# A delta attention in chunks of 32 tokens, and eight experts written out as one sequence

## The chip, the cores and the metric

One core of one Trainium2 chip runs the whole program. The metric is the time on the device in microseconds (us), the median of several executions. Everything is four-byte floating point. A core has five engines, each with an instruction stream of its own: TensorE (PE) multiplies matrices, VectorE (DVE) and ScalarE (ACT) work on elements, GpSimd (POOL) does elementwise work too, and SyncE (SP) starts transfers. They wait for each other by semaphores. On PE each product of four-byte numbers stands in the trace as two matmul records and two weight-load records (PEld); the count of products in the program order is therefore half of the records. A transpose on PE leaves one record of each kind.

## The reference

Four layers, each an attention and a feed-forward part with layernorms and residuals, run over 4 sequences of 1024 tokens and 128 channels (32 tiles of 128 tokens). Two parts matter here. The feed-forward part of layer 2:

```
logits = x @ gate_w.T                  # 8 experts
mult, sel = _sparse_mixer_top2(logits) # two experts per token and their weights
h1, h3 = x @ w1[e].T, x @ w3[e].T      # 256 wide, every expert for every token
out = sum_e weight[t, e] * ((silu(h1) * h3) @ w2[e].T)
```

The attention of layer 3 (4 heads of 32 channels): q, k and v are projections with a convolution of 4 taps and silu; v also goes through convolutions of 7 and of 25 taps; a delta rule runs in chunks of 32 tokens:

```
T = I + strictly lower part, so that T = inverse(I + tril(beta k k^T, -1))
u_i = T v_i - T k_i S                  # per chunk of 32 tokens
o_i = q_i S + tril(q_i k_i^T) u_i
S   = S + k_i^T u_i
```

The four paths (two convolutions, the delta rule's output, v itself) are then mixed by a small router network.

## The kernel before, in words

The program is a row of stages. A stage (`Stage`) allocates buffers and semaphores, has one block with a function for each engine, and ends in a barrier of all engines (`end_step`). Inside a block each engine runs its instructions in the order in which they are written; there is no scheduler. So the order of the code is the order on each engine.

**The experts, `l2_ffn_stage` (L2267 on).** After the weights are loaded and turned, a hardware loop (`nc.Fori`) makes 8 passes, each over 512 tokens. A pass copies its columns of `XNT` to `xs` (ACT), multiplies them with the gate (PE, `logits`), and on VectorE finds the two best experts and their weights in some thirty small operations on 32 columns. Then come 8 experts: for each half k of the hidden width PE makes `h1` and `h3` (128x512), ACT the tanh `th`, VectorE `gated` and `act`; `second_product` makes `y` in 8 products of 128x128; `gather` adds it with its weight to `acc` on VectorE. `h1`, `h3` and `y` have two buffers each. The last operation adds `acc` to `X`. Every pass begins when the pass before it is over on all engines.

**The preparation, `l3_paths_steps` (L2498 on).** It runs once for each of the four sequences: projections (PE), copies (ACT), convolutions of 4 taps (VectorE, one operation of 128x1024 for each tap), silu, then on VectorE the convolution of 7 taps into `lm[:, 0]`, the sums of squares for the norms (`sums`, from small products on PE), reciprocal, the scaled keys `kn_tok`, and the convolution of 25 taps into `lm[:, 1]`. PE turns these to token rows, ACT copies them to `outs`.

**The chunk stage, `l3_chunk_steps` (L2627 on).** It runs once for each pair of sequences (`a3d0`, `a3d1`), after the preparation of the two. A step takes the next 128 tokens of both. Phase q of a step builds a 128x128 gram per head and sequence (`big`), masks it to `N`, cuts out its 32x32 diagonal blocks `Nc`, makes five masked levels `lev` (POOL), and grows the inverse: `SMALL`-1 = 4 rounds on 32x32 blocks in which PE makes `zt`, ACT copies it to `Zt`, PE makes both the new `T` (`tps`) and its transpose (`xps`), VectorE adds them; then two rounds join the blocks to 64 and to 128 (`T64`, `Zt6`, `x5`, `x6`). Phase r takes the previous 128 tokens: `kS`, `R`, `u` (with 128x128 stationary `XT`), the output, and the state `S`, a 128x128 matrix of which only the heads' blocks are kept (`dS`). There are 8 blocks of 128 tokens, so 9 steps.

Of the kernel before, what the change touches and what calls it, by code (L numbers as in the profile page):

```python
# [2266 lines left out]
def l2_ffn_stage(nc, X, XNT, c, gate_w, w1, w2, w3):  # L2267


    with Stage(nc, "f2") as outer:  # L2270
# [11 lines left out]
        with Stage(nc, "f2s") as st:  # L2282
            xs = st.sb("xs", [P, G * P])
            lg, size, gap, first, second, rest = (st.sb(n, [P, G, EXPERTS]) for n in
                                                  ("lg", "size", "gap", "first", "second", "rest"))
# [4 lines left out]
            atf = st.sb("atf", [P, G, 8])  # L2290
            total, mult = (st.sb(n, [P, 2, G]) for n in ("total", "mult"))
# [3 lines left out]
            acc = st.sb("acc", [P, G, P])  # L2295
            logits = st.ps("logits", (P, G, EXPERTS))
            h1 = st.ps("h1", (P, 2, 512))
            h3 = st.ps("h3", (P, 2, 512))
            y = st.ps("y", (P, 2, G, P))
            s = st.sems("xs_ready logits_ready shifted1 exps h1_ready h3_ready th_ready act_ready y_ready y_used "  # L2300
                        "added chain")
            with nc.Fori(0, TILES // G) as i:
                with nc.Block(no_gpsimd_drain=True) as block:
                    @block.scalar
                    def _(a):
                        a.activation(xs[:], XNT[:, ds(i * G * P, G * P)], ACT.Copy).then_inc(s["xs_ready"], 1)
                        a.wait_ge(s["shifted1"], 1)
                        a.activation(ex1[:], ex1[:], ACT.Exp)
                        a.activation(ex2[:], ex2[:], ACT.Exp).then_inc(s["exps"], 1)
                        for n in range(2 * EXPERTS):  # L2310
                            a.wait_ge(s["h1_ready"], n + 1)
                            if n >= 2:
                                a.wait_ge(s["act_ready"], n - 1)
                            a.activation(th[:, n % 2, :], h1[:, n % 2, :], ACT.Tanh, scale=0.5).then_inc(s["th_ready"], 1)
# [1169 lines left out]
```

## Time and profile before

| | |
|---|---|
| median of 3 executions | 8866.54 us (8864.33 to 8873.16) |
| the profiled execution: time / its span | 8869.6 us / 8867.9 us |
| VectorE busy in the experts' stretch 6901 to 7337 | 300 of 436 us |
| 25-tap and 7-tap operations on VectorE (128x1024) | 120 of 1285 ns |
| preparation 7366 to 7442: VectorE / PE busy | 59.6 / 26.8 of 76 us |
| PE waits put to "issue" in 7517 to 7875 | 48.7 us in 40 waits, longest 2.1 us |

Times in the trace count from the span's start. "[1.46 <-issue]" behind an instruction says that its engine had been idle for 1.46 us before it, and what ended the idle time; "issue" means that nothing recorded was waited for. PEclk is the granted clock of PE as a share of 2.4 GHz: 0.5 is its lower level of 1.2 GHz. The experts, the four preparations and the two chunk stages together lie between 6899 us and 8385 us of the span; nothing of another stage runs beside them.

### The profile page before, as it was taken

The page shows a single profiled execution, that of the slowest core. Times are in us where ns is not written, and L with a number is a line of the kernel's source. Part 1 is how long each engine was busy: PE and PEld are TensorE (multiplying, and loading weights), DVE is VectorE, ACT ScalarE, POOL GpSimd, SP SyncE. Part 2 cuts the span into 40 slices and gives each one's busy share as a digit, 9 for nine tenths or more (in the row PEclk, how much of TensorE's full clock was granted, in tenths as well). Part 3 has the DMA queues.
Part 4 walks back from the last instruction along what each step waited for, and adds up shares of the span by engine and source line. Part 5 has one row for each costly group of instructions (what it writes and reads, how often), then busy time and mean ns, then how long its engine had stood idle before and what let it go on. Part 6 is the DMA issues. An engine that isn't in the chain of part 4 may idle for free. (4 is left out here: it accounts for less than half of the span.)

```text
span 8867.9 us, 296237 instructions
## 1 busy us (share of the span) xinstructions
PE 7434.6 (84%) x129602; PEld 5365.8 (61%) x129602; DVE 5896.1 (66%) x11053; ACT 4141.6 (47%) x6986; POOL 2935.6 (33%) x2152
## 2 busy tenths in 40 slices
PE   7999699999996998988988998998986784756666
PEld 3443588888885665665665665666654453645534
DVE  6664477777776885876876866867865667253266
ACT  3554244444444775765765766756752121111121
POOL 0111022222223773764754755746730000101000
PEclk8998699999998998999999999999998895555556
DMA  0000000000001221221221222212210000000000
GB/s 14 1 1 1 5 5 5 5 5 5 5 3 40 70 73 43 69 72 40 73 65 47 70 59 56 71 50 63 72 30 5 9 0 2 3 2 2 4 0 12
DMA packets 192069, 256.75 MB, mean 29 GB/s; under 512 B 59957, under 2 KB 86452, under 8 KB 189876
## 3 DMA queue, kind: packets, MB, share of 16 engines
q1 hardware_dynamic: 190772, 237.70, 10.1%
q8 instruction: 1029, 16.86, 0.8%
q14 instruction: 268, 2.20, 0.1%
HBM read 27.84 MB, written 2.10 MB: 3 GB/s over the span
## 5 line engine op out<-in xcount | busy, mean ns | idle before, releaser
L1764 PE MATMUL wa_front<-w_wqkv,wa_xsT 128*128 128x512 f32 x2000 | 994.8, 621 | 40.1 <-PEq L66 20.3
L1686 POOL TENSOR_TENSOR XNT<-XNT 128x1024 f32<-128x1024 f32 x396 | 937.8, 2368 | 251.2 <-DVE XNT L1870 251.2
L1689 POOL TENSOR_TENSOR XNT<-XNT,wa_rnorm 128x1024 f32<-128x1024 f32 x330 | 627.9, 1903 | 361.9 <-DVE wa_rnorm L1878 361.9
L1867 DVE TENSOR_TENSOR XNT<-wa_front,w_scaled 128x1024 f32<-128x1024 f32 x330 | 393.5, 1192 | 311.1 <-ACT wa_sq L1705 228.8
L1764 PEld LDWEIGHTS wa_front<-w_wqkv,wa_xsT 128*128 128x128 f32 x2000 | 346.3, 193 | 316.9 <-issue 297.4
L446 PE MATMUL a0h_ring<-a0h_QT,a0h_KT 32*128 32x512 f32 (+3 forms) x1536 | 457.5, 567 | 14.2 <-ACT a0h_E L564 10.4
L564 ACT ACTIVATE a0h_E<-a0h_ring 128x512 f32<-128x512 f32 (+1 forms) x640 | 320.6, 555 | 296.7 <-PE a0h_ring L446 295.1
L1705 ACT ACTIVATE wa_sq<-wa_front 128x1024 f32<-128x1024 f32 x335 | 340.1, 1015 | 182.5 <-PE wa_front L1764 182.5
L1870 DVE TENSOR_TENSOR XNT<-wa_front,w_scaled 128x512 f32<-128x512 f32 x660 | 421.0, 679 | 0.0
L1883 DVE TENSOR_REDUCE wa_norm<-wa_sq 128x16 f32<-128x1024 f32 x330 | 398.5, 1207 | 0.0
L1770 PEld LDWEIGHTS wa_front<-consts,XNT 128*128 128x128 f32 x2640 | 299.0, 142 | 124.7 <-issue 62.3
L1770 PE MATMUL wa_front<-consts,XNT 128*128 128x128 f32 x2640 | 357.1, 278 | 14.7 <-POOL XNT L1689 6.9
L1348 POOL TENSOR_TENSOR a1s_Estrict<-a1s_E,a1s_sb 128x512 f32<-128x512 f32 x64 | 81.2, 1269 | 861.3 <-ACT a1s_E L1286 861.3
L437 PE MATMUL a0h_slots<-a0h_KT,a0h_QT 32*128 32x512 f32 (+3 forms) x1536 | 349.1, 559 | 8.6 <-DVE a0h_part L643 3.4
L1908 DVE TENSOR_TENSOR wa_o<-wa_back,wa_rtotal 128x1024 f32<-128x1024 f32 x165 | 202.0, 1224 | 210.9 <-PE wa_back L1826 210.9
L2817 POOL TENSOR_TENSOR a3d_sb<-consts,a3x_nbeta 128x1024 f32<-128x1024 f32 x16 | 31.0, 1937 | 926.9 <-POOLq L66 926.9
L1852 PE MATMUL wa_back<-w_wo,wa_oT 128*128 128x128 f32 x2640 | 330.5, 280 | 5.6 <-ACT wa_oT L1750 5.6
L606 POOL TENSOR_SCALAR_AFFINE_SELECT a0h_E<-a0h_E 128x512 f32<-128x512 f32 x128 | 79.7, 635 | 755.3 <-ACT a0h_E L564 755.3
L1692 POOL TENSOR_TENSOR wa_sc<-wa_sc,wa_smax 128x1024 f32<-128x1024 f32 x160 | 304.3, 1902 | 70.5 <-DVE wa_smax L1921 70.5
L1852 PEld LDWEIGHTS wa_back<-w_wo,wa_oT 128*128 128x128 f32 x2640 | 315.6, 196 | 7.6 <-ACT wa_oT L1750 7.6
L1826 PEld LDWEIGHTS wa_back<-wa_v_look,wa_pT 64*32 64x32 f32 x21120 | 223.0, 106 | 154.3 <-issue 146.9
L1379 DVE SCALAR_TENSOR_TENSOR a1s_conv<-a_hist,a_taps,a1s_conv 128x512 f32<-128x512 f32 x384 | 303.9, 791 | 11.2
(659 smaller groups left out, 19547.7 us busy)
## 6 DMA issues: line engine op xcount, KB each, us to landing
wa_v_look<-wa_v_all SPq DMA_DIRECT2D x990, 128.0 KB, 2.4
wa_v_look<-wa_v_all SPq DMA_DIRECT2D x660, 64.0 KB, 2.0
wal_v_look<-wal_v_all SPq DMA_DIRECT2D x198, 128.0 KB, 2.4
wal_v_look<-wal_v_all SPq DMA_DIRECT2D x132, 64.0 KB, 2.0
w_wqkv<-in_L_ffn_Wqkv_dram SPq DMA_DIRECT2D x6, 1024.0 KB, 6.4
w_wo<-in_L_ffn_Wo_dram SPq DMA_DIRECT2D x6, 512.0 KB, 6.9
w_wqkv<-in_L_ffn_Wqkv_dram SPq DMA_DIRECT2D x12, 256.0 KB, 7.9
f2w_raw<-in_L_ffn_w_dram SPq DMA_DIRECT2D x48, 64.0 KB, 1.9
```

The costliest lines, as they stand in the source:

```text
L437: last = pe.matmul(o[:, i, at:at + w], QT[rows, n % 2, t * P:(t + 1) * P], KT[rows, n % 3, k * 512:k * 512 + w], start=True, stop=True)
L446: last = pe.matmul(o[:, at:at + w], KT[rows, n % 3, kb * P:(kb + 1) * P], QT2[rows, k, 512 - w:512], start=True, stop=True)
L564: a.activation(E[:, m % 3, j, 0:w], ring_of(key)[:, 0:w], ACT.Exp).then_inc(s["ring_a"], 1)
L1686: g.tensor_tensor(rot[:, at], rot[:, at], part[:, at], ALU.add).then_inc(s[summed], 1)
L1689: g.tensor_tensor(rot[:, at], rot[:, at], spread(rnorm[:, at, :], HDW), ALU.mult).then_inc(s[done], 1)
L1705: a.activation(sq[:, n].rearrange("p h d -> p (h d)"), two_banks(front, bank[n]), ACT.Square).then_inc(s[done], 1)
L1764: last = pe.matmul(front[:, first + i, :], xsT[:, slot, :], wqkv[:, (2 * n + i) * 512:(2 * n + i + 1) * 512], start=True, stop=True)
L1770: last = pe.transpose(front[:, first + i // 4, (i % 4) * P:(i % 4 + 1) * P], rot[:, n, 2 * i:2 * i + 2, :].rearrange("p h d -> p (h d)"), ...
L1852: last = pe.matmul(back[:, 0, 0:P], oT[:, i, :], wo[:, i, :], start=(i == 0), stop=(i == INNER // P - 1))
L1867: v.tensor_tensor(rot[:, n], src, cos, ALU.mult)
L1870: last = v.tensor_tensor(part[:, n, :, p0:p0 + 32], src[:, :, p1:p1 + 32], sin[:, :, p0:p0 + 32].broadcast_to([P, H, 32]), ALU.mult)
L1883: v.tensor_reduce(norm[:, n, :], sq[:, n], AX.X, ALU.add).then_inc(s[norm_in], 1)
```

## The change

Three things change.

1. **Experts.** No loop over passes: one block holds 64 units of work (8 groups of 512 tokens by 8 experts) in a row, all reading `XNT` itself. The gate products of all 32 tiles come first, then one routing on 256 columns for all tokens. `y` has three buffers, `gather` adds straight into `X` and stands between the two halves of a later unit.
2. **Preparation.** Keys and values are turned by head (`turn_heads`: 128 products of 32x32 each), the sums of squares come as 8 + 128 + 128 products, the norms' operations stand inside the 25-tap convolution (behind its taps 14 and 18), and the keys stay unscaled: `bp` = beta/|k|^2 takes the norm in.
3. **Chunk stage.** One stage for all four sequences, with chunks of 32 tokens. Partition quarters are heads; a step has M = 16 matrices per quarter (4 chunks by 4 sequences). Gram and scores are one set of 64 products of 32x64 (`gq`). The inverse is `XT` alone, grown 4 times by one set (`xps`); VectorE's 32x32 transpose gives `T` from `XT` (`turn`), so that `tps` and the rounds to 64 and 128 go. The state is 32x32 per head and sequence, carried chunk by chunk (`look`, `solve`, `learn`, 4 times in a step); the output is turned at the step's end (`oT`).

The core of the diff:

```
-            with nc.Fori(0, TILES // G) as i:
+            work = [(g, e) for g in range(NG) for e in range(EXPERTS)]
...
+                    for i in range(len(work)):
+                        hidden(2 * i)
+                        if i >= 2:
+                            gather(i - 2)
+                        hidden(2 * i + 1)
...
-            turn(rawp[:, 0], qk[:, 1, k], s["tok_ps"])
+            turn_heads(rawp[:, 0], qk[:, 1, b], s["ktok_ps"])
...
+            convolve(act[:, 2, :], vh[:], wide_taps[:, LOCAL:], MID, {14: sums, 18: scales}).then_inc(s["path_ready"], 1)
...
-                        blocks_of(tps, XTc, lambda p, m: Zt[p, m, :], s["t_ps"])
-                        blocks_of(xps, Zt, lambda p, m: XTc[p, m, :], s["x_ps"])
+                    each(every, whole(xps), whole(Zt), whole(XT[:, q % 2])).then_inc(s["x_ps"], 1)
...
+                    each(every, lambda p, m: gq[p, m, :, :], chan(1, q),
+                         lambda p, m: qk[p, :, m % BATCH, tokens(q, m)]).then_inc(s["gq_ps"], 1)
+                for n in range(PER):
+                    look(n)
+                    zt(n + 1)
+                    solve(n)
+                    grow(n + 1)
+                    learn(n)
...
+                def turn():
+                    v.wait_ge(s["X_ready"], LX * q + turns + 1)
+                    if LV * q + turns >= 1:
+                        v.wait_ge(s["zt_ps"], LV * q + turns)
+                    v.transpose(columns(T[:]), columns(XT[:, q % 2])).then_inc(s["T_ready"], 1)
...
+                g.wait_ge(s["N_ready"], q + 1)
...
+                for n in range(SMALL):
+                    g.tensor_tensor(lev[:, n], N[:], small[:, n:n + 1, :].broadcast_to(tiny), ALU.mult).then_inc(s["lev_ready"], 1)
```

How it stands on the engines, at three places. First PE in the chunk stage; before, from the last round on 32x32 blocks (`ztp`, `tps`, `xps`) over the joining rounds to the next step's gram and state products (`big`, `rec`):

```order
L2666 MATMUL a3d_ztp<-a3d_T,a3d_lev 32x32 x32
L2666 MATMUL a3d_tps<-a3d_Zt,a3d_XTc 32x32 x32
L2666 MATMUL a3d_xps<-a3d_XTc,a3d_Zt 32x32 x32
L2691 MATMUL a3d_ztp<-a3d_T,a3d_N 32x32 x16
L2718 MATMUL a3d_tps<-a3d_Zt,a3x_XT 32x32 x8
L2722 MATMUL a3d_xps<-a3x_XT,a3d_Zt 32x32 x16
L2699 MATMUL a3d_ztp<-a3x_T,a3d_N 64x64 x8
L2728 MATMUL a3d_xps<-a3x_XT,a3d_Zt 64x64 x8
L2739 MATMUL a3d_big<-a3x_qk 128x128 x8
L2746 MATMUL a3d_rec<-a3x_S,a3x_qk 128x128 x2
L2753 MATMUL a3d_rec<-a3d_R,a3x_XT 128x32 x8
```

and now, in the middle of a run of steps, from the output's transposes over the gram-and-score set to the first state update (`kps` and the first `ops` are `look`, `ups` is `solve`, `sps` and the second `ops` are `learn`):

```order
L2755 MATMUL a3d_ztp<-consts,a3d_oT 128x128 x4
L2673 MATMUL a3d_gq<-a3x_qk 32x64 x64
L2673 MATMUL a3d_kps<-a3d_S,a3x_qk 32x32 x16
L2673 MATMUL a3d_ops<-a3x_qk,a3d_S 32x32 x16
L2673 MATMUL a3d_ztp<-a3d_T,a3d_lev 32x32 x64
L2673 MATMUL a3d_ups<-a3d_R,a3d_XT 32x32 x16
L2673 MATMUL a3d_xps<-a3d_XT,a3d_Zt 32x32 x64
L2673 MATMUL a3d_sps<-a3d_u,XN 32x32 x16
L2673 MATMUL a3d_ops<-a3d_AT,a3d_u 32x32 x16
```

The joining rounds are gone, and the state's products stand between the inverse's in each of the four rounds. A full step of before has 510 products, in 14 such steps and two half ones; now one has 896 and 4 transposes (64, and 4 times the 208 from `kps` to the second `ops`), in 7 such steps; the first step has 576 (no state), the last 320 and 4 transposes (no inverse). Second, VectorE in the preparation, before from the 7-tap convolution on:

```order
L2592 SCALAR_TENSOR_TENSOR a3p_lm<-a3p_vh,a3x_wide_taps,a3p_lm 128x1024 x6
L2610 TENSOR_SCALAR a3p_sums<-a3p_rawp 128x8x2x4
L2612 TENSOR_SCALAR a3x_beta<-a3p_tb 128x32
L2613 TENSOR_SCALAR a3x_nbeta<-a3p_tb 128x32
L2615 RECIPROCAL a3x_rnorms<-a3p_sums 128x64
L2617 TENSOR_TENSOR XN<-a3p_rawp,a3x_rnorms 128x1024
L2590 TENSOR_SCALAR a3p_lm<-a3p_vh,a3x_wide_taps 128x1024
L2592 SCALAR_TENSOR_TENSOR a3p_lm<-a3p_vh,a3x_wide_taps,a3p_lm 128x1024 x24
```

and now:

```order
L2604 SCALAR_TENSOR_TENSOR a3p_act<-a3p_vh,a3x_wide_taps,a3p_act 128x1024 x14
L2623 TENSOR_SCALAR a3x_rnq<-a3p_rawp 128x32
L2624 TENSOR_SCALAR a3p_ss<-a3p_rawp 128x32
L2625 TENSOR_SCALAR a3p_tb<-a3p_tb 128x32
L2604 SCALAR_TENSOR_TENSOR a3p_act<-a3p_vh,a3x_wide_taps,a3p_act 128x1024 x4
L2629 RECIPROCAL a3p_ss<-a3p_ss 128x32
L2630 TENSOR_TENSOR a3x_bp<-a3p_tb,a3p_ss 128x32
L2631 TENSOR_SCALAR a3x_nbp<-a3x_bp 128x32
L2632 RECIPROCAL a3x_rnq<-a3x_rnq 128x32
L2634 TENSOR_TENSOR a_outs<-a3p_rawp,a3p_root 128x8x128
L2604 SCALAR_TENSOR_TENSOR a3p_act<-a3p_vh,a3x_wide_taps,a3p_act 128x1024 x6
```

The small operations that wait for PE's sums stood ahead of the 25-tap convolution and stand inside it now. Third, VectorE at the experts' beginning, where the two experts of each token are found, before, in each of 8 passes:

```order
L2350 COPY f2s_lg<-f2s_logits 128x32
L2352 MAX f2s_top<-f2s_lg 128x8 x4
L2355 MAX_INDEX f2s_at<-f2s_top,f2s_lg 128x8 x4
L2357 TENSOR_SCALAR f2s_size<-f2s_lg 128x32
L2358 CAST f2s_atf<-f2s_at 128x32
L2359 TENSOR_TENSOR f2s_size<-f2s_size,f2s_lg 128x32
```

and now, once:

```order
L2348 COPY f2s_lg<-f2s_logits 128x256
L2350 MAX f2s_top<-f2s_lg 128x8 x32
L2353 MAX_INDEX f2s_at<-f2s_top,f2s_lg 128x8 x32
L2355 TENSOR_SCALAR f2s_size<-f2s_lg 128x256
L2356 CAST f2s_atf<-f2s_at 128x256
L2357 TENSOR_TENSOR f2s_size<-f2s_size,f2s_lg 128x256
```

Eight small routings have become one wide one ahead of all 64 units. Behind it, a unit's instructions on PE and VectorE are those of an expert before, except that the weighted sum stands between the two halves of a unit.

## Rows read from the trace of the kernel before

**Rows 1.** Busy time by stretch; columns: us, each engine's busy time, PEclk, DMA share, GB/s.
```profile
6901.00:7337.00 436.00, 374.94 (x1600) 233.69 (x1600) 300.30 (x856) 91.05 (x159) 0.00 (x0) 0.92 0.00 0
...
6970.00:6985.00 15.00, 15.00 (x72) 9.70 (x71) 10.64 (x23) 2.98 (x5) 0.00 (x0) 0.99 0.00 0
...
8025.00:8384.00 359.00, 259.61 (x8156) 236.55 (x8156) 91.36 (x198) 42.96 (x104) 39.41 (x24) 0.51 0.01 3
```

**Rows 2.** Timeline, experts, even running: start us, us, engine, line, operation, count [idle<-releaser].
```profile
6921.27 1.95 PE L2329 MATMUL f2s_y<-f_w2T,f2s_act 128*128 128x128 f32 x16
...
6926.49 1.95 PE L2329 MATMUL f2s_y<-f_w2T,f2s_act 128*128 128x128 f32 x16
```

**Rows 3.** Timeline of the experts: second pass up to its first activation; stage behind them.
```profile
6956.44 1.88 PE L2320 MATMUL f2s_logits<-f_gT,f2s_xs 128*128 128x8 f32 x8 [5.33 <-ACT f2s_xs L2306]
...
6958.58 0.37 DVE L2352 MAX8 f2s_top<-f2s_lg 128x8 f32<-128x8 f32 x4
...
6959.66 0.18 DVE L2357 TENSOR_SCALAR f2s_size<-f2s_lg 128x32 f32<-128x32 f32 x1
...
6965.06 0.69 DVE L2392 SCALAR_TENSOR_TENSOR f2s_gated<-f2s_th,f2s_h 128x512 f32<-128x512 f32 x1
...
7337.28 1.28 ACT L167 ACT_TABLE_LOAD   x1 [6.92 <-PEq L66]
```

**Rows 4.** The gate products of all eight passes, by tile: ns, first and last start.
```profile
L2320 PE MATMUL f2s_logits<-f_gT,f2s_xs x64: 256/361/382, 6901.3 to 7287.0; 128*128 128x8 f32 x64
```

**Rows 5.** Timeline, preparation of the first sequence.
```profile
7388.66 1.94 PE L2518 MATMUL a3p_rawp<-consts,a3x_qk 128*128 128x128 f32 x8 [15.32 <-DVE a3x_qk L2603]
...
7402.36 0.23 DVE L2610 TENSOR_SCALAR a3p_sums<-a3p_rawp 128x64 f32<-128x64 f32 x1 [2.73 <-ACT a3p_tb L2568]
...
7403.85 0.55 DVE L2615 RECIPROCAL a3x_rnorms<-a3p_sums 128x64 f32<-128x64 f32 x1 [1.09 <-ACT a3p_sums L2570]
...
7438.07 1.97 PE L2518 MATMUL a3p_mid<-consts,a3p_lm 128*128 128x128 f32 x8 [28.68 <-DVE a3p_lm L2592]
```

**Rows 6.** Timeline, where chunk stages begin and the stages behind them begin.
```profile
7517.98 1.24 PE L2739 MATMUL a3d_big<-a3x_qk 32*128 32x128 f32 x16 [2.02 <-PEq L66]
...
7873.81 4.55 PE L2523 MATMUL a3p_rawp<-XNT,a3x_proj 128*128 128x512 f32 x5 [1.64 <-PEq L66]
...
8025.55 1.24 PE L2739 MATMUL a3d_big<-a3x_qk 32*128 32x128 f32 x16 [1.97 <-PEq L66]
...
8384.94 0.33 SPq L2932 DMA_DIRECT2D a3y_rw1a<-in_L_attn_r_w_dram  x1
```

**Rows 7.** Timeline of TensorE in the second chunk stage, dense 32x32 products.
```profile
8306.57 0.26 PE L2666 MATMUL a3d_ztp<-a3d_T,a3d_lev 32*32 32x32 f32 x8 [1.46 <-issue]
...
8310.14 0.34 PE L2666 MATMUL a3d_xps<-a3d_XTc,a3d_Zt 32*32 32x32 f32 x9 [1.45 <-issue]
8310.27 1.06 PE L2666 MATMUL a3d_ztp<-a3d_T,a3d_lev 32*32 32x32 f32 x64
8311.83 0.96 PE L2666 MATMUL a3d_tps<-a3d_Zt,a3d_XTc 32*32 32x32 f32 x55 [0.50 <-ACT a3d_Zt L2805]
8313.63 0.37 PE L2666 MATMUL a3d_tps<-a3d_Zt,a3d_XTc 32*32 32x32 f32 x9 [0.83 <-issue]
...
8321.21 0.27 PE L2666 MATMUL a3d_xps<-a3d_XTc,a3d_Zt 32*32 32x32 f32 x5 [1.46 <-issue]
```

**Rows 8.** The page, busy time and instructions of each engine, then its queues.
```profile
PE 7434.6 (84%) x129602; PEld 5365.8 (61%) x129602; DVE 5896.1 (66%) x11053; ACT 4141.6 (47%) x6986; POOL 2935.6 (33%) x2152
...
q8 instruction: 1029, 16.86, 0.8%
```

**Rows 9.** Timeline, GpSimd's masks in a chunk step.
```profile
7604.36 0.72 POOL L2824 TENSOR_TENSOR a3d_lev<-a3d_Nc,a3x_small 128x256 f32<-128x256 f32 x1 [38.97 <-ACT a3d_Nc L2792]
7605.04 2.35 POOL L2825 TENSOR_TENSOR a3d_lev<-a3d_Nc,a3x_small 128x1024 f32<-128x1024 f32 x1
```

**Rows 10.** Groups by line in the experts: xcount, busy us, mean ns, idle us, releaser.
```profile
L2314 ACT ACTIVATE f2s_th<-f2s_h 128x512 f32<-128x512 f32 x128 | 75.4, 595 | 234.5 <-PE f2s_h L2338 234.5
```

More of the change, by code:

```diff
@@ L2425 @@
+            st.end_step()
 HEADS3 = 4
@@ L2474, in _ @@
             def _(v):
-                v.memset(XT[:], 0.0)
-                v.memset(T64[:], 0.0)
+                for i, mask in enumerate((c.strict, c.upto)):
+                    for h in range(HEADS3):
+                        v.tensor_copy(within[quarter(h), i, 0, :], mask[quarter(h), quarter(h)])
                 v.wait_ge(s["loaded"], 160)
@@ L2508, in l3_paths_steps @@
     mine = slice(b * BLOCKS, (b + 1) * BLOCKS)
+    QS, KS, BS = (slice(n * CHUNKS3, (n + 1) * CHUNKS3) for n in range(3))
     def by_tile(ap):
@@ L2519, in turn, with turn_heads @@
                 last.then_inc(sem, 1)
+            def turn_heads(out, src, sem):
+                for n in range(CHUNKS3):
+                    at = slice(n * CHUNK3, (n + 1) * CHUNK3)
+                    for h in range(HEADS3):
+                        last = pe.matmul(out[quarter(h), at], src[quarter(h), at], c.ident[quarter(h), quarter(h)], start=True,
+                                         stop=True)
+                last.then_inc(sem, 1)
             for n in range(3):
@@ new lines, in grow, with look @@
+                    pe.wait_ge(s["zt_ready"], LV * q + n)
+                    pe.wait_ge(s["X_ready"], LX * q + n)
+                    each(every, whole(xps), whole(Zt), whole(XT[:, q % 2])).then_inc(s["x_ps"], 1)
+                def look(n):
+                    if r is None:
+                        return
+                    k = PER * r + n
+                    ms = range(n * BATCH, (n + 1) * BATCH)
+                    pe.wait_ge(s["S_ready"], k + 1)
+                    each(ms, per_batch(kps), chan(1, r), per_batch(S)).then_inc(s["k_ps"], 1)
+                    if n == 0 and r >= 1:
+                        pe.wait_ge(s["o_kept"], r)
+                    each(ms, whole(ops), per_batch(S), chan(0, r), first=ms[0], end=M)
@@ L2781, in _ @@
+                if r is not None:
+                    pe.wait_ge(s["o_kept"], r + 1)
+                    if q is not None:
+                        pe.wait_ge(s["zt_ready"], LV * (q + 1))
+                    for b in range(BATCH):
+                        last = pe.transpose(ztp[:, b * BATCH:(b + 1) * BATCH, :].rearrange("p a e -> p (a e)"), oT[:, b, :], c.ident)
+                    last.then_inc(s["turned"], 1)
         @block.scalar
```

714 lines of the change are left out of this document (312 added, 402 removed).

## The prediction

> **What bounds the kernel now.** I read the busy times by stretch first. Three stretches matter, one after the other with barriers between: the experts (6899 to 7337 us), four preparations of a sequence (about 76 us each) and two chunk stages. Among the experts PE is at 15.00 of 15 us once it runs evenly, at the upper clock level (granted 0.99), but over all passes at 375 of 436 us and 0.92 [rows 1]. In the chunk stage PE is at 260 of 359 us at the lower level (0.51), VectorE at 91, so no engine is full there: the reader has to ask what each round waits for. The timelines give that.
>
> Experts: one expert costs 5.22 us, from one `y` to the next [rows 2]. A pass takes (7287.0 - 6901.3)/7 = 55.1 us [rows 4], 8 x 5.22 = 41.8 of it work; the other 13.3 are the copy to `xs`, the gate products, VectorE's routing (6958.35 to 6965.06) and the restart of PE at the lower clock level [rows 3].
>
> Preparation: VectorE is the chain. It waits twice for PE's and ACT's small sums, 2.73 and 1.09 us [rows 5].
>
> Chunk stage: between its 32x32 sets PE is idle for "issue", 0.8 to 1.5 us each time [rows 7]. Between two such gaps stand 9 + 64 + 55 = 128 matmul records, that is 64 products, each time the same. The page has 129602 matmul and as many load records and 1029 packets of instructions of 16.4 KB each [rows 8]: 252 records to a packet, so a packet is about 64 products. PE has used up its instructions and waits for the next packet. From gap end to gap end it takes 3.57 us, and over four such intervals 8306.57 to 8321.21, 3.66 each [rows 7], the last two of them 3.79. The 64 products themselves take no more than 1.7 us (64 records in 1.06 us, their tail of 0.2 included), and ACT waits of 0.5 us that fall inside an interval do not lengthen it. So dense small products come at one packet per 3.66 us, whatever PE could do. Before, only five of the eight packets of a step (510 products) are that dense; the rest of its 45 us (359.4/8, [rows 6]) is a chain of waits.
>
> At this place a rule speaks against me. The Trainium skill, page "Runtime: NRT & Kernel Launch", section "Instruction fetch mechanics", says that the sequencer fetches the next 16 KiB block of 256 instructions while it runs the present one, that crossing a block is "mostly hidden", and that kernels prefer full unrolling. Size and count of a block agree with the trace; hidden it is not, by gaps of 0.8 to 1.5 us. By the rule the chunk stage would end earlier; that is the first rival below.
>
> **Chunk stage, worked out.** Removed: both stages, 7517.98 to 7873.81 and 8025.55 to 8384.94 [rows 6], 355.8 + 359.4 = 715.2 us. Added, in packets of 64 products: the first step 576 products, seven steps of 896 and 4 transposes, the last 320 and 4.
> - A full step is 14.03 packets, at 3.66 that is 51.4 us. Does the chain fit below? A set of 64 products takes 1.75 us plus 0.2 tail (twice the 64 records above). ACT's 512-wide copy costs 0.60 [rows 10], a 512-wide VectorE operation 0.69 [rows 3]. A round: `look` 0.9, `zt` 1.75, tail, copy and handovers 0.95, `grow` 1.75 + 0.25, VectorE's add 0.7, transpose 0.7, state 0.3 + 0.1: 7.4 us for 208 products, whose 3.25 packets take 11.9. So it fits and the fetch sets the pace; `solve` and `learn` lie beside the copies.
> - VectorE's 32x32 transpose has no row. Below it can't be free, since it reads and writes 512 columns; I take 0.7, as the 512-wide operations. From above, the slowest VectorE row by element is the reciprocal, 0.55 us for 64 columns [rows 5], which would be 4.4 us for 512: the round becomes 11.1 and still fits, the first step (128 products to a round, 7.3 us by packets, then 9.9 by chain) does not: + 10 there and + 4 at each full step's start, + 38 in all. The Trainium skill, "VectorE: DVE Perf Modes", section "The three transpose paths", has 311 ns for 128x128 of two bytes; four times that is an estimate of 1.2 us, and no term would change by it.
> - A step's start does not fit wholly: `gq`, then mask `N` 0.7, POOL's first level (256 columns take 0.72, 1024 take 2.35 [rows 9], so about 1.3 for 512), identity 0.7, transpose 0.7, handovers 0.4: 4 us in which PE has only `look` (0.9) to do. With the packet of `gq` itself, that is 1 us over the packets' time, and the wait for the copy before the output's transposes adds 1. I take 53.5 for a full step; bounds 51.4 (all hidden) and 60 (below). The added waits are `zt`'s for the levels and the transposes' for `o_kept`; behind both stands the whole next set of PE.
> - Sum: first step 9 packets + 1.5 = 34.5; 7 x 53.5 = 374.5; last step 5.03 packets = 18.4, then copy 0.8, transposes 0.9, scaling 0.8, barrier 1.3: 22.3. Together 431.3. Gain 715.2 - 431.3 = 283.9 us. POOL has 7.5 us of work in a step, and VectorE about 12: neither bounds.
>
> **Experts, worked out.** Gone: seven starts. New: gate products of 32 tiles, 64 records; at the lower level 8 take about 1.7 us [rows 3], all 14.2; at the upper, by `y`'s 16 in 1.95 [rows 2], 7.2. The clock rises on the way, I take 10. Then routing: maximum and index of 4 tiles take 6958.58 to 6959.66, 1.08 us [rows 3], 8 times that is 8.6; 21 further operations of 256 columns, between 0.22 each (like the 32-wide) and 0.69 (512-wide), midway 0.45: 9.5; copy 0.3. Together 18.4 (13.5 to 23.4). Then 64 units: first activation to first `y` 6.7, 62 x 5.22 = 323.6, the last two `y` 3.6, the last sum 1.3: 335.3. Barrier 1.2. From 6899.4 on: 10.2 + 18.4 + 335.3 + 1.2 = 365.1, end at 7264.5 where it was 7337.28 [rows 3]: gain 72.8, bounds 63 to 81. Nothing new binds in a unit: the second half's activation ends about 5.7 us after PE has begun the unit, PE asks for it at 6.9. The `xs` copy, its table load and the add into `X` go with the passes.
>
> **Preparation, worked out.** VectorE loses the waits of 2.73 and 1.09 us and starts its 25 taps at 7399.6; `sums` comes behind 0.75 + 14 x 1.285, at 7418.4. PE needs to have: 128 products by head from 7388.66 [rows 5] (two packets, 5.5 to 7.3 us), 8 wide ones 3.4, 256 small ones (four packets 14.6, up to 20.7): 7412 to 7420. Then 8 transposes 2, 128 products 5.5 to 7.3: 7420 to 7429, where `scales` asks at 7424.9. So 25 taps end 4.2 us earlier or up to 4 later than that; I take 3.5 us gained for each of four, 14 us, bounds 0 to 17. The cover is the 25 taps: without them the 14.6 us of packets would be on the path.
>
> **Sum.** Against the profiled execution's own 8869.6 us: 8869.6 - 283.9 - 72.8 - 14 = 8498.9. The median of the runs is 3.1 us lower: 8496 us.
>
> **The rivals.**
> 1. *The fetch is hidden, the chain bounds* (the page's rule). For: nothing but the "issue" gaps shows the fetch, and PE did run 215 records without one behind a slow stretch. Against: every dense stretch of every step has the gaps. Then a full step is 36.5 us (7.4 to the first `zt`, three rounds of 7.3, a last of 5.3, 1.9 for the output), the first 30, the last 17: 302 in place of 431. Time 8367 us. 12%.
> 2. *Waits and fetch add up.* If packets are asked for only as PE gets on, each round's own waits (0.5 for the copy, 1.1 for state and transpose) come on top: + 6.5 in a full step, 60 us, + 10 in the others. For: a packet is fetched only after the packet before is begun. Against: the 0.5 us waits inside the intervals of rows 7. About + 57: 8553 us. 14%.
> 3. *The transpose costs by element like the reciprocal:* + 38, 8534 us. 3%.
> 4. *Slower than before.* The place is the packet fetch: 112.2 packets in the chunk stage. If a fetch took twice as long, because PE's stream in one long stage runs ahead of nothing, 112.2 x 3.66 = 411 us more come on top, and the preparations' small products (384 more in each, 6 packets) outlast the 25 taps: about 8930 us. It decides from 3.66 + 371/112.2 = 7.0 us a packet on. Against: the longest pair of intervals in rows 7 is 3.79 each. 2%.
>
> **How the numbers follow.** My forecast has 69%: 8496, with its own range 8465 to 8530. Range: rival 2 and 3 fall within 8555; below, rival 1 is mostly left out, with the experts' and transposes' bounds I go to 8440. Faster by over 0.2% (18 us, about what a measurement can tell from no change) are all cases but the last: 0.97; no change 0.01; slower 0.02.
>
> **What would show it.** In the new profile: "issue" gaps on PE throughout the chunk stage, 128 matmul records apart, 3.6 to 3.7 us from end to end; full steps of 53 to 54 us; one stage of about 431. Among the experts, `y` every 5.22 us for 335 us at a clock of 0.99, ahead of it 28 to 29 us of gate products and routing. In the preparation, the last turn 3 to 4 us earlier. Wrong would be: no gaps and steps below 45 us (rival 1), steps near 60 with waits for VectorE between gaps (rival 2), `y` further apart than 5.3 us, or `scales` waiting for over 4 us.

## The result and the profile after

| | before | after |
|---|---|---|
| median | 8869.85 us (4 runs) | 8508.15 us (8501.87 to 8527.02, 4 runs) |
| after / before | | 0.9595, 95% interval 0.9578 to 0.9612 |
| predicted | | 8496, range 8440 to 8555 |
| profiled execution | 8869.6 us | 8527.0 us, span 8525.3 |

The change takes 362 us away; the prediction said 374. The profiled execution lies 19 us above the median: its expert stage begins 15.9 us later than in the profile of before (6915.2 against 6899.3), although the code ahead of it is the same. In the fourteen profiles of this case that point lies anywhere from 6880 to 6915 us. So a stage is compared by its own length, and stage lengths tell more than times of whole executions.

The page answers to [rows 8]: PE has 1960 matmul records more in all (fewer for the joining rounds, more for small products), and 26 instruction packets more.

```profile
PE 7158.4 (84%) x131562; PEld 5126.3 (60%) x131562; DVE 5768.2 (68%) x10639; ACT 4064.7 (48%) x6793; POOL 2917.3 (34%) x2152
...
q8 instruction: 1055, 17.29, 0.9%
```

Busy time by stretch, columns as in [rows 1]: the experts, and the seven full steps of the chunk stage. PE is now busy 350 of 366 us among the experts (375 of 436 before), and in the chunk stage still only 216 of 388, still near the lower clock level.

```profile
6914.00:7280.00 366.00, 350.31 (x1600) 224.76 (x1600) 253.09 (x634) 78.20 (x131) 0.00 (x0) 0.96 0.00 1
7633.00:8021.00 388.00, 215.84 (x12561) 195.64 (x12552) 86.66 (x168) 20.56 (x35) 52.39 (x41) 0.53 0.02 4
```

Timeline of the experts: gate products, their copy, VectorE's first activation behind the routing, two `y` in a row, and the first instruction of the stage behind. They answer to [rows 2, 3].

```profile
6915.23 11.54 PE L2316 MATMUL f2s_logits<-f_gT,XNT 128*128 128x8 f32 x64 [1.27 <-PEq L66]
...
6926.81 0.42 DVE L2348 COPY f2s_lg<-f2s_logits 128x256 f32<-128x256 f32 x1 [12.52 <-PE f2s_logits L2316]
...
6943.49 0.69 DVE L2389 SCALAR_TENSOR_TENSOR f2s_gated<-f2s_th,f2s_h 128x512 f32<-128x512 f32 x1
...
6950.21 1.95 PE L2326 MATMUL f2s_y<-f_w2T,f2s_act 128*128 128x128 f32 x16
...
6955.43 1.95 PE L2326 MATMUL f2s_y<-f_w2T,f2s_act 128*128 128x128 f32 x16
...
7280.10 1.28 ACT L167 ACT_TABLE_LOAD   x1 [6.32 <-PEq L66]
```

Gate products 11.5 us (10 predicted), routing 16.7 from the copy to the first activation (18.4), units and last sum 335.7 (335.3), `y` every 5.22. From its first instruction, a table load of ScalarE at 6915.19, to the first of the next stage it takes 7280.10 - 6915.19 = 364.9 us (365.1), against 437.9 before: 73.1 us gained (72.8).

VectorE in the preparation, in answer to [rows 5]: the first tap, `sums`, `scales`, and the first tap of the next sequence. Neither `sums` nor `scales` has idle time ahead of it.

```profile
7313.74 0.75 DVE L2600 TENSOR_SCALAR a3p_act<-a3p_raw,a3x_taps 128x1024 f32<-128x1024 f32 x1 [4.70 <-ACT a3p_raw L2565]
...
7361.56 0.19 DVE L2623 TENSOR_SCALAR a3x_rnq<-a3p_rawp 128x32 f32<-128x32 f32 x1
...
7367.13 0.35 DVE L2629 RECIPROCAL a3p_ss<-a3p_ss 128x32 f32<-128x32 f32 x1
...
7385.95 0.76 DVE L2600 TENSOR_SCALAR a3p_act<-a3p_raw,a3x_taps 128x1024 f32<-128x1024 f32 x1 [4.70 <-ACT a3p_raw L2565]
```

One sequence to the next: 72.2 us, before 75.9. The gain of 3.7 us each was predicted as 3.5. PE's last gates and last turned values, on which the two depend:

```profile
7354.18 0.70 PE L2548 MATMUL a3p_rawp<-a3x_wb,XNT 128*32 128x1 f32 x37 [1.86 <-issue]
...
7361.12 0.68 PE L2523 MATMUL a3p_rawp<-consts,a3p_vh 32*32 32x32 f32 x45 [1.95 <-issue]
```

The small products are done at 7354.9, 6.7 us before `sums` asks, and the values by head at 7361.8, 5.3 us before `scales`.

TensorE in the first step of the chunk stage, up to the second step's first product. It answers to the starts in [rows 6]:

```profile
7597.45 3.36 PE L2673 MATMUL a3d_gq<-a3x_qk 32*32 32x64 f32 x128 [1.97 <-PEq L66]
7605.57 1.93 PE L2673 MATMUL a3d_ztp<-a3d_T,a3d_lev 32*32 32x32 f32 x128 [4.76 <-DVE a3d_T L2806]
...
7612.47 1.93 PE L2673 MATMUL a3d_ztp<-a3d_T,a3d_lev 32*32 32x32 f32 x128 [1.72 <-DVE a3d_T L2806]
...
7632.53 0.30 PE L2673 MATMUL a3d_gq<-a3x_qk 32*32 32x64 f32 x3
```

No state is looked at here, so each round has 128 products; from one `ztp` to the next it takes 6.9 to 7.4 us, and the waits for `T` show between them: this step is in the main a chain of waits. A full step has both, a wait at its start and packets behind it. The rows are: the last packet of the step before, this step's `gq`, VectorE's addition of the identity and its transpose, the first `ztp`, then four gaps (three that follow each other, and the ninth behind them):

```profile
7797.33 0.32 PE L2673 MATMUL a3d_ops<-a3d_AT,a3d_u 32*32 32x32 f32 x5 [1.54 <-issue]
...
7799.39 3.10 PE L2673 MATMUL a3d_gq<-a3x_qk 32*32 32x64 f32 x128
...
7804.64 1.74 DVE L2850 TENSOR_TENSOR a3d_XT<-a3d_lev,a3x_small 128x512 f32<-128x512 f32 x1 [0.58 <-POOL a3d_lev L2789]
...
7806.40 0.71 DVE L2806 STREAM_TRANSPOSE a3d_T<-a3d_XT 128x512 f32<-128x512 f32 x1
...
7807.22 1.93 PE L2673 MATMUL a3d_ztp<-a3d_T,a3d_lev 32*32 32x32 f32 x128 [4.14 <-issue]
...
7811.44 1.65 PE L2673 MATMUL a3d_xps<-a3d_XT,a3d_Zt 32*32 32x32 f32 x106 [1.06 <-issue]
...
7815.19 0.37 PE L2673 MATMUL a3d_sps<-a3d_u,XN 32*32 32x32 f32 x10 [1.82 <-issue]
...
7818.53 1.65 PE L2673 MATMUL a3d_ztp<-a3d_T,a3d_lev 32*32 32x32 f32 x107 [1.16 <-issue]
...
7853.46 0.44 PE L2673 MATMUL a3d_ops<-a3d_AT,a3d_u 32*32 32x32 f32 x16 [1.81 <-issue]
```

The gap of 4.14 us ahead of 7807.22 carries the word "issue" too, but it is a wait for `T`: the transpose ends at 7807.11, and the first `ztp`, which reads `T`, begins 0.1 us later. It does so in each of the seven full steps, and 180 records, not 128, lie between this row and the next gap. The other gaps are those of packets. From 7811.44 to 7853.46 there are 11 intervals of 128 records (127 in some), 42.0 us, 3.82 each. Over all intervals of 128 records in the seven full steps the mean is 3.74, and 3.63 to 3.67 in four other profiles of the same stage; in [rows 7] it was 3.66. The three packets from 7797.33 to 7811.44, over the step's start, take 14.1 us. Last, where the step without an inverse begins, and the next stage:

```profile
8022.44 0.65 PE L2673 MATMUL a3d_kps<-a3d_S,a3x_qk 32*32 32x32 f32 x32
...
8042.24 0.33 SPq L2903 DMA_DIRECT2D a3y_rw1a<-in_L_attn_r_w_dram  x1
```

The chunk stage takes 8042.24 - 7597.45 = 444.8 us, where the two of before took 715.2; predicted were 431.3. PE's waits in the seven full steps (us in total, times, longest):

```profile
PE a3d_ztp L2673 <- issue: 63.0, 29, 4.1
PE a3d_xps L2673 <- issue: 39.3, 28, 2.2
...
PE a3d_kps L2673 <- DVE a3d_S L2832: 10.2, 11, 0.9
PE a3d_xps L2673 <- ACT a3d_Zt L2767: 5.4, 20, 0.3
PE a3d_ztp L2755 <- ACT a3d_oT L2772: 4.2, 6, 0.7
PE a3d_ztp L2673 <- DVE a3d_T L2806: 3.9, 1, 3.9
```

With the groups left out, 148 of 172 us of idle time are put to "issue". But 24 of these are six of the waits for `T` at a step's start, 3.6 to 4.1 us each; for the seventh the profile names `T` (3.9). So 124 us are left for the packets, and handovers come to 47 us, 6.8 a step, four of them at the start. VectorE's and GpSimd's operations on 512 columns, by tile, with the shortest, median and longest in ns:

```profile
L2806 DVE STREAM_TRANSPOSE a3d_T<-a3d_XT x32: 711/711/712, 7604.7 to 8007.6; 128x512 f32<-128x512 f32 x32
...
L2850 DVE TENSOR_TENSOR a3d_XT<-a3d_lev,a3x_small x8: 1731/1734/1735, 7602.9 to 7971.7; 128x512 f32<-128x512 f32 x8
...
L2789 POOL TENSOR_TENSOR a3d_lev<-a3d_N,a3x_small x40: 1256/1263/1718, 7601.6 to 7975.7; 128x512 f32<-128x512 f32 x40
```

The transpose, for which no row of before stood, takes 0.711 us (0.7 was taken). The addition of the identity (L2850) takes 1.73 us where 0.7 was taken. GpSimd's level takes 1.26 (1.3 was taken).

### The profile page after: what moved, and what is told of

The parts are those of the page before. It is cut to its first block and busy times, and to the rows that moved or that the text cites. A ratio compares the mean times of both kernels' runs of the same rounds, so it can differ in the third digit from the quotient of the medians.

```text
span 8525.3 us, 299038 instructions
## 1 busy us (share of the span) xinstructions
PE 7158.4 (84%) x131562; PEld 5126.3 (60%) x131562; DVE 5768.2 (68%) x10639; ACT 4064.7 (48%) x6793; POOL 2917.3 (34%) x2152
## 5 line engine op out<-in xcount | busy, mean ns | idle before, releaser
L446 PE MATMUL a0h_ring<-a0h_QT,a0h_KT 32*128 32x512 f32 (+3 forms) x1536 | 457.3, 567 | 14.2 <-ACT a0h_E L564 10.4
L1379 DVE SCALAR_TENSOR_TENSOR a1s_conv<-a_hist,a_taps,a1s_conv 128x512 f32<-128x512 f32 x384 | 304.3, 792 | 11.2
L643 DVE TENSOR_REDUCE a0h_part<-a0h_slots 128x2 f32<-128x1024 f32 (+3 forms) x256 | 257.3, 1021 | 78.5 <-PE a0h_slots L437 76.3
```

The costliest lines, as they stand in the source:

```text
L446: last = pe.matmul(o[:, at:at + w], KT[rows, n % 3, kb * P:(kb + 1) * P], QT2[rows, k, 512 - w:512], start=True, stop=True)
```

## Experiments

My theory: PE's instruction packets (16 KB, 256 instructions, that is 64 products of four-byte numbers) set the pace of the chunk stage, at a rate that neither the products' own time nor short waits change. Rival: its chain of waits does, with or without the packets' time on top. All names and shapes below are those of the changed kernel; "step" is a full step, a mean over the seven.

### Each part alone

The new `l2_ffn_stage` in the kernel before (`experts_alone`), and the old one in the changed kernel (`layer3_alone`); whole functions are exchanged.

> The kernel before with the new expert stage alone. My theory: the three parts add up, and this one is worth the 73.1 us that lie between the stage's start and its end in the two profiles (437.9 before, 364.9 after): 8870 - 73 = 8797 us. Rival: part of it belongs to what stands behind (code laid out elsewhere, a layernorm that begins at another clock level), then 8810 or more. In its profile the stage should again take 364 to 366 us, with a second product every 5.22 us.

Measured: ratio 0.9925 (0.9907 to 0.9942), 8791.7 us against 8854.0 on the same chip. The stage takes 7271.0 - 6903.1 = 367.9 us, 2 to 4 more than expected. Twelve profiles have this stage: in six it takes 364.9 us and the gate products 11.2 to 11.5, in the other six 367.9 to 368.0 and the gate products 13.8. So most of the 3 us lies in the gate products. Over them the granted clock is 0.50 in `experts_alone` and 0.61 in the changed kernel's profile; the prediction had 14.2 us for the lower clock level.

> The changed kernel with the old expert stage. My theory: 8870 - 270 (chunk stages 715.2 to 444.8) - 15 (preparations) = 8585 us. Rival: the parts depend on each other, for instance because the clock level carries over from the experts into the preparation; then the two savings measured alone differ from the whole, 362, by more than 8 us.

Measured: ratio 0.9689 (0.9666 to 0.9712), 8572.8 us. Chunk stage 435.5 us, preparations 288.3 from the first to the chunk stage (288.6 in the changed kernel, 303.4 before).

By the ratios the parts are worth 67 and 276 us, together 343, the whole 359. The difference of 16 us is more than the 8 that were set as the sign of a dependence; but each figure has an uncertainty of 15 to 20 us, so the totals neither show nor exclude one. The stages' own lengths are sharper: 70 to 73, 15, and 270 to 280 us.

### Fewer products, the same chain

```diff
-                    if n == 0 and r >= 1:
-                        pe.wait_ge(s["o_kept"], r)
-                    each(ms, whole(ops), per_batch(S), chan(0, r), first=ms[0], end=M)
```

> The changed kernel without the 16 products of q S in each round, 64 in each step with a state: this part of the output is left out; the chain of waits for the inverse and the state is the same. Fetch sets the pace: one packet of 64 products less in seven full steps and in the last, 8 x 3.66 to 8 x 3.85, 29 to 31 us less than the changed kernel (8508), 8477 to 8479, and full steps of 52.3 us where they take 56.3 now. Rival, the chain of waits sets it: these products stand beside VectorE's R, at most 0.43 us each round is PE's own time, 32 x 0.43 = 14 us at most and more likely none: 8494 to 8508.

The wait for `o_kept` that goes with them costs nothing: the transposes of the step before have waited for the same copy.

Measured: 8490.3 us (ratio 0.9580, 0.9561 to 0.9599, the changed kernel 0.9595); the stage 417.4 us, a step 52.0. Against three profiles of the unchanged stage (444.8, 435.5, and 436.3 in `after_again`; mean 438.9, step 54.8) that is 21.5 us less, 27.4 against the first alone. The same stage also stands in two runs below, `fetch_micro` (438.2) and `loop_sizes` (443.7); the mean of all five is 439.7, the step again 54.8. The gaps of TensorE stand as before:

```profile
7805.03 1.22 PE L2673 MATMUL a3d_xps<-a3d_XT,a3d_Zt 32*32 32x32 f32 x74 [0.70 <-issue]
...
7809.05 0.36 PE L2673 MATMUL a3d_ops<-a3d_AT,a3d_u 32*32 32x32 f32 x10 [2.10 <-issue]
```

8 packets of 3.7 would be 29 us, the rival's most is 14. Neither fits well: removed packets bring 2.7 us each. An account that fits, made afterwards and not tested by itself: from a step's `gq` to its first `ztp` 8.4 us pass with and without the products of q S (means of seven steps), because the chain for `T` sets the time there. One of the four sets that were left out stood in this stretch and brought nothing. The other three are 0.75 packets, by 3.68 us 2.8 a step, and a step has become 2.8 shorter.

### A longer chain, the same products

```diff
+                    v.transpose(columns(spare[:, (LV * q + turns) % 2]), columns(XT[:, q % 2]))
                     v.transpose(columns(T[:]), columns(XT[:, q % 2])).then_inc(s["T_ready"], 1)
```

> The changed kernel with VectorE's 32x32 transpose done twice each time (the first into a tile that nobody reads), 0.71 us more in the chain of each of 32 rounds, nothing more for PE. Fetch sets the pace and waits shorter than it are covered: only the four rounds of the first step and the start of each of seven full steps show it, 11 x 0.71 = 8 us: 8516, with full steps of 56 to 57. Rival, waits and fetch add up: 32 x 0.71 = 23 us, 8531, full steps of 59. Rival, the chain alone sets the pace: also 23 us, but without a gap every 128 records.

Measured: 8515.3 us (0.9606, 0.9586 to 0.9626). The added operation, by tile, is there 32 times:

```profile
L2809 DVE STREAM_TRANSPOSE a3d_spare<-a3d_XT x32: 711/711/712, 7572.6 to 7974.9; 128x512 f32<-128x512 f32 x32
```

22.8 us of VectorE work lie in the chain. The stage takes 444.1 us, 5.2 above the mean of three, 4.4 above that of five, and 0.7 below the longest; a step takes 55.4 (54.8). From `gq` to the first `ztp` 9.0 us pass instead of 8.4: there the added operation shows, and the step is longer by no more than that. The first step takes 36.6, in the five unchanged profiles 34.4 to 37.7; its three rounds from one `ztp` to the next take 7.4 to 7.9 us for 6.9 to 7.4 above. Of the rival's 59 a step nothing is seen. Behind a step's start the packets cover 0.7 us a round.

### The fetch by itself

A stage ahead of the chunk stage, with products that wait for nothing:

```diff
+        names = [(32, 512), (64, 512), (128, 512), (256, 256), (512, 128)]
...
+                for w, count in names:
+                    for i in range(count):
+                        p = quarter(i % 4)
+                        pe.matmul(outs[w][p, 0:w], qk[p, 1, 0, 0:32], qk[p, 0, 0, 0:w], start=True, stop=True)
...
+        with nc.Fori(0, 6) as i:
...
+                    for i in range(256):
```

> The changed kernel with a stage of its own ahead of the chunk stage, whose products wait for nothing: 512 products with a 32x32 stationary and 32 moving columns, 512 with 64, 512 with 128, 256 with 256, 128 with 512, 192 of 128x128, and then a hardware loop that makes the same 256 products of 32x32 six times. Theory A, the fetch of a packet runs beside the products of the packet before: a packet takes the larger of 3.7 us and its products' own time. 32 columns: 3.7 a packet (own time 1.9); 64 columns: still 3.7 (own time 3.4); 128 and more: own time, no gaps. Theory B, a packet is asked for only when the one before is used up: own time + 1.9 us each time: 3.8, 5.3 with 64 columns, 8 to 9 with 128, gaps in all of them. Loop: if instructions that were fetched stay, its passes from the second on take 256 products' own 7.6 us, otherwise 14.8.

TensorE's timeline: 32 moving columns; 64 at the lower clock level; 64 at the upper; 128 and more; then the loop, its first pass and its third.

```profile
7584.35 1.93 PE L2659 MATMUL mic_w<-a3x_qk 32*32 32x32 f32 x128 [1.54 <-issue]
...
7598.78 6.26 PE L2659 MATMUL mic_w<-a3x_qk 32*32 32x64 f32 x256 [1.39 <-issue]
...
7609.47 1.99 PE L2659 MATMUL mic_w<-a3x_qk 32*32 32x64 f32 x128 [1.48 <-issue]
...
7628.19 82.75 PE L2659 MATMUL mic_w<-a3x_qk 32*32 32x128 f32 x1766 [1.33 <-issue]
...
7761.99 1.93 PE L2677 MATMUL mil_loop<-a3x_qk 32*32 32x32 f32 x128 [1.54 <-issue]
...
7775.36 4.49 PE L2677 MATMUL mil_loop<-a3x_qk 32*32 32x32 f32 x512 [1.37 <-PEq L66]
```

With 32 columns a packet comes every 3.47 us (three of seven 3.75) though its products take 1.93. With 64 columns at the lower level (granted clock 0.50 from 7570 to 7600) two packets run without a gap between them, 3.13 us each; near the upper (0.93 from 7605 to 7628) the same products take 1.99 and the next packet still comes after 3.5 to 4.0. From 128 columns on no gap is left. So theory A holds: the fetch runs beside the products, and a packet takes the larger of the two. No effect of the clock level on the fetch is seen. The surprise is the loop: its first pass has gaps, each later pass makes its 256 products (4 packets) without one, the second in 5.5 us and the others in 4.5. In these passes the instruction queue moves no packet at all, in the first it moves four. The next run asked how long a loop may be.

```diff
+    for count in (384, 480, 544, 640, 896):
...
+            with nc.Fori(0, 3) as i:
```

> The changed kernel with a stage ahead of the chunk stage, of hardware loops of three passes each, whose bodies are 384, 480, 544, 640 and 896 products of 32x32: 6, 7.5, 8.5, 10 and 14 packets of instructions. A body of 4 packets ran at 3.47 us a packet in its first pass and at 1.12 in the later ones. Theory: instructions stay until their room is needed, so that bodies up to some size run without gaps from the second pass on, and longer ones at 3.5 us a packet in every pass; a step of the chunk stage (14 packets) then is too long to gain by a loop. Rival: only what the loop's last four packets hold stays, then all five show gaps in each pass.

TensorE's timeline: a packet of the first pass of 384 products, the second and third pass; a packet in the first pass of 480 products, one in its second:

```profile
7593.66 1.93 PE L2657 MATMUL lo_out<-a3x_qk 32*32 32x32 f32 x128 [1.54 <-issue]
...
7604.15 8.86 PE L2657 MATMUL lo_out<-a3x_qk 32*32 32x32 f32 x768 [1.66 <-PEq L66]
7614.45 6.68 PE L2657 MATMUL lo_out<-a3x_qk 32*32 32x32 f32 x768 [1.45 <-PEq L66]
...
7626.27 1.42 PE L2657 MATMUL lo_out<-a3x_qk 32*32 32x32 f32 x128 [2.32 <-issue]
...
7657.12 1.93 PE L2657 MATMUL lo_out<-a3x_qk 32*32 32x32 f32 x128 [2.75 <-issue]
```

384 products (6 packets) make their later passes without a gap and without a packet on the instruction queue, in 8.9 and 6.7 us; 480 (7.5 packets) and all longer bodies have their gaps in every pass, and 4.6 to 4.9 us of idle time at each way back, where the loops that fit have 1.4 to 1.7. In the longest body 13 packets take 7991.26 - 7943.40 = 47.9 us: 3.68 each, the undisturbed rate. The Trainium skill, page "Runtime: NRT & Kernel Launch", section "Instruction fetch mechanics", gives PE room for 128 KiB of instructions, which is 8 packets; further down it says that the room is only two blocks, for 32 KiB. For PE, 6 packets that stay and 7.5 that don't fit the first and not the second. It also says that kernels prefer full unrolling. For these streams the measurement differs: 256 products take 5.9 us in a loop that fits, the way back included, and 13.9 or more unrolled.

### Versions with fewer products

Two pairs of products share their stationary operand, `S` and `u`, and can be one product with 64 moving columns. `look_merged` does it for `S`:

```diff
-                    each(ms, per_batch(kps), chan(1, r), per_batch(S)).then_inc(s["k_ps"], 1)
-                    each(ms, whole(ops), per_batch(S), chan(0, r), first=ms[0], end=M)
+                    each(ms, lambda p, m: look_ps[p, m % BATCH, :, :], per_batch(S),
+                         lambda p, m: qk[p, :, m % BATCH, tokens(r, m)]).then_inc(s["k_ps"], 1)
...
+                    v.transpose(kT[:], look_ps[:, :, 1, :]).then_inc(s["kT_ready"], 1)
```

and `both_merged` for `u` too, with keys and scores side by side in one tile `AK`:

```diff
-                    each(ms, per_batch(sps), lambda p, m: k_tok[p, k, m % BATCH, :], per_batch(u)).then_inc(s["s_ps"], 1)
-                    last = each(ms, whole(ops), per_batch(u), whole(AT[:, r % 2]), first=M, end=ms[-1])
+                    each(ms, lambda p, m: ops[p, m, :, :], per_batch(u),
+                         lambda p, m: AK[p, r % 2, m, :, :]).then_inc(s["s_ps"], 1)
...
+                    v.transpose(dS[:], ops[:, n * BATCH:(n + 1) * BATCH, 1, :]).then_inc(s["dS_ready"], 1)
```

> The changed kernel with k S and q S as one product with 64 moving columns (S stationary): 832 products to a full step in place of 896. In exchange VectorE turns k S once a round (128 columns, about 0.3 us), ACT copies q S (0.25 us), and the sum of the two parts of the output moves from PE to VectorE. Fetch theory: 8 packets less, 8 x 3.4 to 8 x 3.85 = 27 to 31 us off the changed kernel: about 8480. Rival, the chain sets the pace: 32 x 0.3 us more on it and nothing off: 8508 to 8518.

> The kernel of look_merged with the state's and the output's products of u also as one with 64 moving columns (u stationary, beside it the output's scores and the keys in one tile, ACT copies the keys there once a step, 0.6 us; VectorE turns the state's update, 0.3 us a round): 768 products to a full step, 12 packets in place of 14. Fetch theory: 16 packets less, 54 to 62 us off the changed kernel: 8446 to 8454, full steps of 49. Rival, the chain: 8520 to 8528.

`look_merged` took 8472.5 us where 8480 was expected. `both_merged` took 8478.2 where 8446 to 8454 were expected; its full steps took the expected 49. Both were run again with the changed kernel on one chip:

> The changed kernel unaltered, as the measure for the two below on the same chip. 8500 to 8515 us; in its profile a chunk stage between 435 and 445 us, as in the two profiles of the same stage so far (435.5, 444.8).

> The kernel of look_merged again. Fetch theory, by its profiled stage (423.3 us where two profiles of the stage with 896 products have 435.5 and 444.8, mean 440.1): 17 us below the changed kernel on the same chip; by 8 packets of 3.6 us 29 us below.

> The kernel of both_merged again. Its time was 6 us above look_merged's although its chunk stage was 23.5 us shorter (399.8), because the stages ahead of the experts, whose code is the same, took 27 us longer in its profile. Theory: these stages scatter by up to 33 us from one execution to the next whatever stands behind them, and over more rounds this kernel comes out 20 us below look_merged and 40 to 50 below the changed kernel. Rival: the length of the code behind moves the stages ahead for good, and it stays within 8 us of look_merged.

| kernel | products in a step | chunk stage, us | step, us | ratio to before (95%) |
|---|---|---|---|---|
| changed | 896 | 444.8 | 55.7 | 0.9595 (0.9578 to 0.9612) |
| the same again | 896 | 436.3 | 54.4 | 0.9597 (0.9579 to 0.9615) |
| look_merged | 832 | 423.3 | 52.6 | 0.9554 (0.9534 to 0.9575) |
| the same again | 832 | 420.1 | 52.1 | 0.9573 (0.9553 to 0.9592) |
| both_merged | 768 | 399.8 | 49.0 | 0.9562 (0.9542 to 0.9581) |
| the same again | 768 | 404.7 | 49.6 | 0.9557 (0.9538 to 0.9576) |

On that chip the three took 8507.1, 8485.2 and 8468.0 us: 22 and 39 us less, where 17 to 29 and 40 to 50 were expected. `both_merged` beats the changed kernel, its stage is 37 us shorter in the mean. Its first time, 6 us above `look_merged`, came from the stages ahead, which took 27 us longer in its profile than in that of `look_merged`, and did not come again (8455.7 in the second profile, with a stage of 404.7); that it beats `look_merged` is shown by the stage (19 us), not by the totals, whose intervals overlap. But 16 packets less bring 2.3 us each and not 3.7. PE's waits in its full steps, in the second profile, say where the rest is:

```profile
PE a3d_xps L2679 <- issue: 41.3, 28, 2.8
PE a3d_ztp L2679 <- issue: 36.8, 15, 4.3
PE a3d_look L2679 <- DVE a3d_S L2848: 25.5, 21, 1.7
```

"Issue" has shrunk, though six waits for `T` of 3.8 to 4.3 us are in it here too, and the state is waited for: 25.5 us, where the changed kernel had 10.2. Each removed set of 16 products was paid with 0.3 us of VectorE in the state's path.

### VectorE's slow addition

```diff
                 for n in range(SMALL):
+                    if n == 1:
+                        g.wait_ge(s["X_ready"], LX * q + 1)
                     g.tensor_tensor(lev[:, n], N[:], ...
```

> The kernel of both_merged, in which GpSimd waits with its levels 1 to 4 until VectorE has added the identity to level 0. In every profile so far that addition takes 1.73 to 1.75 us where other 128x512 additions of VectorE take 0.69, and GpSimd works on levels beside it. Theory, the two disturb each other: the addition falls to 0.69, the next set of products then waits for level 1 (1.26 us after the addition) in place of the transpose, 0.5 us earlier than now, a step: the stage 4 us shorter (398 to 403). Rival, the addition is slow for its operands (two that are read from SBUF, one of them broadcast): it stays at 1.73, level 1 comes later, and the stage is 4 us longer or more.

Measured: 8484.7 us (0.9558, 0.9541 to 0.9576), the stage 403.5, a step 49.5. The addition, in ns:

```profile
L2868 DVE TENSOR_TENSOR a3d_XT<-a3d_lev,a3x_small x8: 677/678/692, 7592.6 to 7925.7; 128x512 f32<-128x512 f32 x8
```

It falls from 1.73 to 0.68 us, so GpSimd's work beside it was the cause. The wait that is now the last at a step's start, in the full steps:

```profile
PE a3d_ztp L2679 <- POOL a3d_lev L2802: 25.0, 7, 3.8
```

As expected, PE now waits there for level 1. From `gq` to the first `ztp` 7.9 us pass, in the two profiles of `both_merged` 8.3 and 8.5: most of the expected 0.5 us a step is there. It does not show in the stage, whose length scatters by more (399.8 and 404.7).

## Why the prediction was right, and where it was off

- **Experts, right.** 364.9 us for 365.1, in part by luck: the gate products are 1.5 longer and the routing 1.7 shorter than taken, which cancels, and in six of the twelve profiles the gate products are 2.3 us longer still. The routing's 256-column operations take 0.42 us; midway, 0.45, was a fair choice.
- **Preparation, right.** 3.7 us a sequence for 3.5. PE's small products came at the early end of the bounds, and the cover was never short.
- **Chunk stage, right in its mechanism, 13.5 us short in its size** (8.4 against the mean of five profiles). First step 35.1 for 34.5. Last step 19.8 for 22.3. The mis-sized term is the full step, 55.7 (mean of three 54.8) for 53.5, and in it the start, for which the prediction added 2.1 us to the packets' time. Where the records show three packets over a step's start, they take 14.3 us (mean of 22 in five profiles), 3.3 more than 3 x 3.68 and 1.2 more than foreseen. In this chain stands the identity, 1.73 us for the 0.7 that the prediction took. The packets behind the start come at 3.63 to 3.67 us in four of the profiles, so the waits inside are hidden, as predicted; only in the profiled execution of the result are they slower, 3.74, 0.9 us a step, for a reason that no run shows.
- **Packets:** 112.2 were predicted for the stage; the instruction queue moved 113 in it:

```profile
q8 instruction: 113, 1.85, 1.8%
```

- **Rival 1, a hidden fetch** (302 us for the stage), is out: the gaps are there, and a bare stream has them. What the Trainium skill says in the section named above, "mostly hidden", holds here only from 128 moving columns on.
- **Rival 2, waits and fetch add up** (60 us a step), is out in its full size, by `turn_twice2`: 0.7 us more in each round's chain costs 5 us in the stage at most, not 23. A part of it is true: at a step's start a longer chain does show, and a removed packet brings only 2.2 to 2.7 us. (The extra time of this rival adds up to 55.5 us, 7 x 6.5 + 10, and not 57; nothing hangs on it.)
- **Rival 3, a slow transpose,** is out: 0.711 us.
- **The identity,** 1.73 for 0.7 us, eight times, is on the chain that PE waits for at each step's start. How much of the 1.2 us by which the start was mis-sized comes from it is not shown: `both_pool` takes it away and `ztp` comes some 0.4 us a step earlier, not 1.0, since PE then waits for GpSimd's next level.
- **The total.** Terms of the profiled stages: 73.1 + 14.8 + 270.4 = 358.3 us, and 15.9 us of later start stand against it in that execution; the medians differ by 362. The forecast of 374 is off by the chunk stage's 13.5, less 1.1 from the other two parts. An error of this size can be read from the stages and not from single executions, since the stages ahead scatter by 34 us.

What stays open: why the five identical chunk stages scatter by 9 us and the stages ahead by 34. The mean transfer of an instruction packet is 1.12 and 1.10 us in the two longest of the five stages (444.8 and 443.7) and 1.06 to 1.07 in the other three, which could explain 6 us of it, but no run tests that. And whether the steps could run as a hardware loop: a step has 14 packets, a round 3.3, so only a loop over rounds would fit. That wasn't tried.

## What to carry to other kernels

Before small products are made smaller or more numerous, count PE's instructions: where 64 products of four-byte numbers (256 instructions) take less than 3.7 us, the count sets the time and not the work, and the trace shows it as "issue" gaps every 128 matmul records. Count the records between two gaps before calling one a fetch, and look whether another engine's result that PE needs ends just ahead of it: the longest "issue" gaps of this stage were such waits. A product that is removed from a stretch where the chain sets the time brings nothing. Elsewhere merge products that share the stationary operand, or put them in a loop of at most 6 packets. Then compare stages by their own length in the profiles, since whole executions scatter by more than such an edit is worth.

## What the runs showed of the hardware

- Where nothing is waited for, an instruction packet of 16 KB (256 instructions) comes to PE every 3.47 to 4.02 us, in steps of about 0.27; the mean is 3.68 over 13 packets of `loop_sizes` and 3.59 over 7 of `fetch_micro`. With 32 moving columns at granted clock 0.50 and 64 at 0.93 it is the same.
- A loop whose body is 4 or 6 packets isn't fetched again (no packet on the instruction queue in its later passes); one of 7.5, 8.5, 10 or 14 packets is, in every pass.
- VectorE's addition of two 128x512 operands in SBUF takes 1.73 us beside GpSimd's work and 0.68 us without; one such operation of GpSimd takes 1.26. Its 32x32 transpose of 128x512, which reads one, takes 0.71 us in both cases. The Trainium skill, page "SBUF — State Buffer", section "Terms", has a port pair that the two engines share and hold for a full instruction; these rows agree.
- VectorE's 32x32 transpose takes 0.71 us for 512 columns and 0.27 to 0.32 us for 128 columns read from PSUM.
